# Diagonal matrices of x from a ring in DRAM in place of two engines' products

## The reference, cut to what matters

```python
xw = jnp.einsum('ntd,dh->nth', x, Wx) + b
def step(prev_h, xw_t):
    next_h = jnp.tanh(xw_t + prev_h @ Wh)
    return (next_h, next_h)
_, hs = jax.lax.scan(step, h0, jnp.swapaxes(xw, 0, 1))
```

## Time and profile before

| | us |
|---|---|
| median of 3 runs | 3383.85 |
| lowest and highest | 3377.65, 3384.16 |
| the profiled execution | 3381.28 |
| its span | 3379.5 |
| recurrence, first h_now to last | 12.8 to 2043.9 |
| VectorE busy | 2809.4 (83%) |
| GpSimd busy | 2593.7 (77%) |
| ScalarE busy | 2171.9 (64%) |
| TensorE busy | 2812.6 (83%) |

### The profile page before, as it was taken

How to read it: one execution, slowest core, us unless ns; L and a number is a source line. 1 busy time by engine, 2 the same in 40 slices (tenths; PEclk the granted TensorE clock), 3 DMA queues, 4 the chain that set the end, 5 groups by cost and what they waited for, 6 DMA issues and landing times.

```text
span 3379.5 us, 54177 instructions
## 1 busy us (share of the span) xinstructions
PE 2812.6 (83%) x12991; PEld 1717.5 (51%) x13101; DVE 2809.4 (83%) x8061; ACT 2171.9 (64%) x4492; POOL 2593.7 (77%) x2804
## 2 busy tenths in 40 slices
PE   5777778777787877878777788969999999999997
PEld 2333333333333333333333336746767777777676
DVE  5999999999999999999999994337777777777875
ACT  4666666666666666666666663336666666666665
POOL 8888888888888888888888881038778778778773
PEclk9999999999999999999999998879999999999999
DMA  1000000000000000000000002000010101000000
GB/s 33 0 0 0 0 0 0 0 0 0 0 0 0 0 0 0 0 0 0 0 0 0 0 0 73 1 1 1 0 36 0 36 0 36 0 32 4 0 0 7
DMA packets 21860, 21.97 MB, mean 7 GB/s; under 512 B 6334, under 2 KB 19396, under 8 KB 21060
## 3 DMA queue, kind: packets, MB, share of 16 engines
q1 hardware_dynamic: 21828, 21.55, 2.0%
HBM read 21.02 MB, written 0.52 MB: 6 GB/s over the span
## 4 chain that ended last, share of the span: by engine, by line
DVE 54%; PE 21%; issue 15%; ACT 4%; POOL 3%; DVEq 2%; SPq 0%; DMA 0%; POOLq 0%; ACTq 0%
DVE bank L1017 13%; PE bank L1322 5%; DVE bank L1012 3%; DVE bank L989 3%; DVE rot_s L1235 3%; DVE sq L989 3%; DVE rot_c L1235 3%; DVE ss L1238 3%; PE bank L1564 2%; DVE qT L998 2%; PE bank L1642 2%; DVE fix_trace L1083 2%; PE bank L1426 2%; PE bank L1616 2%; DVE sq L1075 2%
## 5 line engine op out<-in xcount | busy, mean ns | idle before, releaser
L1017 DVE TENSOR_REDUCE bank<-qkv_w 128x2 f32<-128x766 f32 (+1 forms) x768 | 912.7, 1219 | 120.6 <-issue 64.9
L739 ACT COPY qkv_w<-bank 128x512 f32<-128x512 f32 x258 | 218.2, 846 | 356.9 <-PE bank L1322 356.9
L667 POOL TENSOR_TENSOR qk<-rot_c,rot_s 128x512 f32<-128x512 f32 x192 | 256.8, 1337 | 207.8 <-DVE rot_s L1235 207.8
L1322 PE MATMUL bank<-diag_h,w_part 128*128 128x512 f32 x1024 | 307.2, 421 | 118.2 <-DVE bank L1012 106.9
L585 POOL TENSOR_TENSOR diag_h<-eye,part 128x512 fp32r<-128x512 f32 x384 | 393.9, 1040 | 0.0
L578 POOL TENSOR_TENSOR qkv_w<-b,offset 128x512 f32<-128x512 f32 x258 | 269.1, 1043 | 160.4 <-ACT b L721 150.0
L1327 PE MATMUL bank<-kT,wx 128*128 128x512 f32 x516 | 277.0, 618 | 136.3 <-ACT b L721 136.3
L1322 PE MATMUL bank<-diag_x,w_part 128*128 128x512 f32 x1032 | 385.6, 495 | 0.0
L1337 PE MATMUL bank<-qT,wh 128*128 128x256 f32 (+1 forms) x768 | 254.6, 467 | 95.6 <-DVE qT L998 95.6
L674 POOL TENSOR_TENSOR rs<-rs,halfs 128x8 f32<-128x8 f32 x192 | 320.1, 1667 | 16.0
L716 ACT ACTIVATE diag_x<-eye,X 128x128 fp32r<-128x128 f32 x1036 | 327.7, 389 | 1.4 <-DVE X L1110 1.4
(11 more groups left out here) (237 smaller groups left out, 6697.5 us busy)
## 6 DMA issues: line engine op xcount, KB each, us to landing
qkv_w<-in_L_ffn_Wqkv SPq DMA_DIRECT2D x6, 1536.0 KB
o_w<-in_L_ffn_Wo SPq DMA_DIRECT2D x6, 512.0 KB
w<-in_L_ffn_W SPq DMA_DIRECT2D x6, 341.0 KB
b<-in_L_ffn_b SPq DMA_DIRECT2D x6, 341.0 KB
w<-in_L_ffn_W SPq DMA_DIRECT2D x6, 128.0 KB
x_tok<-in_x SPq DMA_DIRECT2D x1, 512.0 KB
masks<-in_masks SPq DMA_DIRECT2D x1, 512.0 KB, 3.8
out<-o_fin SPq DMA_DIRECT2D x1, 512.0 KB, 3.2
```

What stands on the lines that cost most here:

```text
L667: pool.tensor_tensor(o, c_, s_[:, :, ::-1, :], ALU.add).then_inc(rot_sum, 1)
L1017: return dve.tensor_reduce((sum_h, sum_x)[n][:, a:b], chain[n][:, a:b, 0:LINKS], AX_X, ALU.add)
L1322: return pe.matmul(dst, w_part[:, n, w], diag[n][:, d, a:b, :].rearrange("p n k -> p (n k)"), start=start, stop=stop or n == 0, skip_group ...
```

## The change

`diag_x` is no longer computed. A tensor in DRAM, `diag_ring`, holds four slots of the tile's shape. VectorE clears the tile once, and SyncE stores the zeros to all four slots. Then, for a step of x, two DMAs write only the diagonals' elements, 128 x 8 for each part, 4 bytes at a time, a row of the tile and one column apart; the off-diagonal zeros stay. Two DMAs per step (one for each half of the batches, both parts at once, 512 KB) load a slot into `diag_x`. The first four steps are sent ahead of the loop, one after another; in the loop the sends run four steps ahead. ScalarE's and GpSimd's `diag_x` instructions go, in the prologue and in the loop, with the counters that found their slices. TensorE waits for the load of a half in place of the two engines.

```diff
+RING = 4
+        ring = nc.dram_tensor('diag_ring', (RING, P, 2, NB, D), F32, kind='Internal').ap()
@@ sync
+            def send_diagonals_x(step, slot):
+                for d in range(2):
+                    src = x_part[d][:, step, :] if isinstance(step, int) else x_part[d][:, bass.ds(step, 1), :].rearrange(
+                        "p a n -> p (a n)")
+                    dst = bass.AP(ring.tensor, (slot * P * 2 + d) * NB * D, [[2 * NB * D + 1, P], [D, NB], [1, 1]])
+                    sp.dma_start(dst, src.unsqueeze(2), allow_slow_non_contiguous=True).then_inc(diag_x_sent, 16)
+            def bring_diagonals_x(slot, half):
+                rows = slice(4 * half, 4 * half + 4)
+                sp.dma_start(diag[1][:, :, rows, :].bitcast(F32), ring[slot][:, :, rows, :]).then_inc(diag_x_ready[half], 16)
+            sp.wait_ge(diag_x_clear, 1)
+            for slot in range(RING):
+                sp.dma_start(ring[slot], diag[1].bitcast(F32)).then_inc(ring_clear, 16)
+            sp.wait_ge(x_split, 1)
+            sp.wait_ge(ring_clear, 16 * RING)
+            for slot in range(RING):
+                if slot:
+                    sp.wait_ge(diag_x_sent, 32 * slot)
+                send_diagonals_x(slot, slot)
+            for half in range(2):
+                bring_diagonals_x(0, half)
+            sp.wait_ge(rest_ready[1], 1)
+            bring_diagonals_x(1, 0)
+            with sp.Fori(0, T // RING) as turn:
+                for u in range(RING):
+                    t = RING * turn + u
+                    sp.wait_ge(rest_ready[1], value(sp, 2 * t + 2))
+                    bring_diagonals_x((u + 1) % RING, 1)
+                    sp.wait_ge(rest_ready[1], value(sp, 2 * t + 3))
+                    bring_diagonals_x((u + 2) % RING, 0)
+                    sp.wait_ge(diag_x_sent, value(sp, 32 * t + 32 * RING))
+                    send_diagonals_x(value(sp, (t + RING) % T), u)
@@ gpsimd
-            pool.wait_ge(x_split, 1)
-            for half in range(2):
-                diagonal(1, 1, half, lower_x(0, half), diag_x_ready[1])
...
-            pool.wait_ge(rest_ready[1], 1)
-            diagonal(1, 1, 0, lower_x(1, 0), diag_x_ready[1])
...
-                pool.wait_ge(rest_ready[1], counts[1])
-                diagonal(1, 1, 1, lower_x(around, 1), diag_x_ready[1])
...
-                pool.wait_ge(rest_ready[1], counts[2])
-                diagonal(1, 1, 0, lower_x(beyond, 0), diag_x_ready[1])
@@ scalar
-                diagonals_x(0, half)
-            diagonals_x(1, 0)
-                diagonals_x(around, 1)
-                diagonals_x(beyond, 0)
@@ vector
+            dve.memset(diag[1].rearrange("p a n k -> p (a n k)").bitcast(F32), 0.0).then_inc(diag_x_clear, 1)
@@ tensor
-            def rests_x(half, count):
+            def rests_x(half, count, landed):
...
+                pe.wait_ge(diag_x_ready[half], landed)
                 for d in range(2):
-                    pe.wait_ge(diag_x_ready[d], count)
                     times(at, 1, 0, d, a, b, False, False)
...
+            pe.wait_ge(diag_x_ready[0], 16 * T + 32)
+            pe.wait_ge(diag_x_sent, 32 * (T + RING))
```

More of the change, by code:

```diff
@@ L307, in program @@
         diag_lower_h = [sem("diag_lower_h%d" % half) for half in range(2)]
-        diag_x_ready = [sem("diag_upper_x"), sem("diag_lower_x")]
+        diag_x_ready = [sem("diag_x%d" % half) for half in range(2)]
+        diag_x_clear = sem("diag_x_clear")
+        diag_x_sent = sem("diag_x_sent")
+        ring_clear = sem("ring_clear")
         tri_h_first = sem("tri_h_first")
@@ L586, in diagonal @@
                                    values.unsqueeze(2).to_broadcast([P, 4, D]), ALU.mult).then_inc(done, 1)
-            def lower_x(m, half):
-                return x_part[1][:, m, 4 * half:4 * half + 4] if isinstance(m, int) else x_part[1][
-                    :, bass.ds(m, 1), 4 * half:4 * half + 4].rearrange("p a n -> p (a n)")
             def at_step(m):
@@ L611, in _ @@
                 counts = [value(pool, two + n) for n in (1, 2, 3, 4)]
-                around, beyond = (value(pool, (t + n) % T) for n in (1, 2))
                 pool.wait_ge(h_static, this)
@@ L711, in lower_h @@
                 ins.then_inc(diag_lower_h[0], 1)
[L713 to L717, removed]
             def take_sums_x(half, count):
@@ L761, in _ @@
                 counts = [value(act, two + n) for n in (1, 2, 3, 4)]
-                around, beyond = (value(act, (t + n) % T) for n in (1, 2))
                 place_guess_h(0, counts[0])
@@ L1364, in _ @@
             sums_x(1, 2)
-            rests_x(0, 1)
+            rests_x(0, 1, 16)
             pe.wait_ge(rest_placed[1], 1)
-            rests_x(1, 2)
+            rests_x(1, 2, 16)
             offset_h()
@@ L1371, in _ @@
                 counts = [value(pe, two + n) for n in (1, 2, 3, 4)]
+                landed = value(pe, 16 * t + 32)
                 for m in range(2):
@@ L1392, in _ @@
                 pe.wait_ge(rest_placed[1], counts[1])
-                rests_x(0, counts[2])
+                rests_x(0, counts[2], landed)
                 pe.wait_ge(guess_placed, counts[1])
@@ L1397, in _ @@
                 pe.wait_ge(rest_placed[1], counts[2])
-                rests_x(1, counts[3])
+                rests_x(1, counts[3], landed)
             def transposed(dst, src, cols, n, done):
```

## The result

| | before | after |
|---|---|---|
| median, us | 3383.85 (5 runs) | 3402.89 (5 runs) |
| lowest and highest | 3377.65, 3386.61 | 3395.32, 3405.14 |
| profiled execution, its span | 3381.28, 3379.5 | 3395.32, 3393.5 |
| first tanh scan, last tanh scan | 55.4, 2043.5 | 73.6, 2061.4 |
| TensorE's first matmul behind the recurrence | 2046.81 | 2064.95 |

The ratio is 1.0055, with a 95% interval of 1.0039 to 1.0070: slower by 0.55%, or 19.0 us between the medians. The profiled execution of after is the fastest of its five. Its recurrence ends 18.1 us later than before's (2064.95 against 2046.81), while its whole span is only 14.0 us longer. The other 4.1 us came back in the stages behind, whose code is the same, and the medians don't show that gain. The comparison is therefore made inside the recurrence.

A forecast was written before the change was run, and what follows sets the result against it. VectorE's row of instructions was taken to bound the loop, 14.69 of 15.67 us a turn. Prologue terms 12.4 - 0.3 + 2 = +14.1 us on the 3383.9 median gave 3398, range 3388 to 3424.

The forecast's parts named there:

- The steady turn: what goes: In the loop, ScalarE loses 2.54 us and GpSimd 2.08 us a turn; nobody on VectorE's row waits for either, value 0.
- The steady turn: what comes: In the loop, each turn's two 512 KB loads and the element sends stay hidden behind 14.2 us of cover, value 0.
- The stall bound: In the loop, traffic stops being hidden when a turn's sends take 12.7 us, or 99 ns a descriptor.
- The clears: In the prologue, four 1 MB stores of zeros start at 19.5 us, take 12.0 plus 0.5, and land at 32.0.
- A slot: In the prologue, each send waits for the landing before it and takes 3.3 us; three of them reach 41.9.
- The load: In the prologue, half 0's load takes 3.8 us, plus 0.6 behind the fourth send's elements, landing at 47.5.
- The slow matmuls: In the prologue, TensorE runs about half of its first rests slowly after some 12 us idle: +2 us (0 to 4).
- L716 out of the chain: In the prologue, ScalarE's 0.96 us `diag_x` instruction leaves the chain of waits: -0.3 us, between 0 and -1.0.
- The end: At the recurrence's end, the last sends, issued at about 2040, land within 5 us and delay the next stage by 0.
- Dear sends: Rival, chance 0.18: an element store costs 50 ns, 6.4 us a send; four on the prologue's path add 18 us, 3416.
- Ready sooner: Rival, chance 0.13: the prologue's ring is ready sooner, or scatter covers the delay; about +5 us, 3389.
- The loop gets faster: Rival, chance 0.07: GpSimd's `diag_x` products hold up VectorE's tanh; removing them returns 67 us over 128 turns, 3331.

The follow-up runs named there:

- e1: Kernel before, with the `diag_x` products of steps 1 to 127 left out on both engines and no ring; 3382.65 us, ratio 1.0005.
- e2: Kernel before with all its products, plus the whole ring traffic loaded into two unused tiles, TensorE waiting for the loads; 3401.98 us, ratio 1.0059.
- e6: Kernel after with seven further sends a turn into a tensor nobody reads, 8 in all; 4811.23 us, 26.48 us a turn.
- e7: Kernel after with eleven further sends a turn into a tensor nobody reads, 12 in all; 6203.24 us, 37.32 us a turn.
- e3: Kernel after, with step 0 sent and loaded before the other three slots are filled; 3389.63 us, ratio 1.0026.
- e5: Kernel after with zeros written first, ring DMAs issued ahead of later stages' loads, slot 0 first, last four sends dropped; 3384.91 us, ratio 1.0000.
- e4: Kernel after, with 17 extra matmuls keeping TensorE busy just ahead of its wait for the first load; 3399.42 us, ratio 1.0054.
- e12: Kernel of e8 with only the three tanh tiles `f_keep`, `f_guess` and `fix_keep` moved from PSUM to SBUF; 3801.48 us, ratio 1.1244.
- e10: Kernel of e8, no ring, with two more VectorE tanh instructions on ScalarE and three tanh tiles moved from PSUM to SBUF; 3741.39 us, ratio 1.1050.
- e9: Kernel of e5, the ring with the lean prologue, with VectorE's second h-triangle instruction made on ScalarE; 3340.40 us, ratio 0.9869.
- e8: Kernel before, no ring, with VectorE's second h-triangle instruction (0.33 us) made on ScalarE; 3341.78 us, ratio 0.9876.
- e11: Kernel of e9, with the ring, two more VectorE tanh instructions on ScalarE and three tanh tiles in SBUF; 3564.28 us, ratio 1.0533.

## Why the prediction was right

The time forecast, 3398.0, is 4.9 us under the median, inside the range and inside the likeliest case's own bounds (3394 to 3405).

**The steady turn: what goes is worth 0.** Right, and shown: e1 is 15.656 a turn with the products gone. ScalarE is at 8.28 where 8.0 was forecast, and GpSimd at 11.23 where 11.2 was.

**The steady turn: what comes costs 0.** Right, and shown by e2. The lengths inside the hidden part were too short. A load lands in 5.3 us, not 3.8, and an element costs 21 ns when the queues are full, not 14; both were within their cover of 14.2 us. The stall bound of 12.7 us of sends a turn was too high. At 2.7 us for a send, e6 and e7 both leave 4.8 us of their turns for all else, where the bound took 3.0. By them an old turn of 15.65 has room for 10.8 us, or four sends (an estimate; no run has between one and eight).

**The clears: 19.5 + 12.0 + 0.5 = 32.0.** Landed at 29.75. The stores ran at 387 GB/s where 350 was taken, and they were under way at the start of the window from 20 us, so that term was 2.2 too long.

**A slot: 3.3 us.** The first of two mis-sized terms. The sends are issued at 29.83, 34.42, 38.63 and 43.09, 4.4 us apart, so three cost 13.3 in place of 9.9. It was put together from a load into SBUF, which landed 2.3 us after its issue. The store into DRAM takes 3.8 to 4.1 from its second issue. The queues carry the first send's data until 32.1 us by their packets, and it lands at 34.40, 2.3 later: the greater part of the wait is behind the data.
The Trainium skill, page "DMA: Bandwidth & Descriptors", section "Anatomy of one DMA — SWDGE (gpsimd) path", says for another issuing path that most of some 2 us of fixed cost is the wait until the target memory confirms the last write, most of all in DRAM; the 2.3 us here agree in size.

**The load: 3.8 + 0.6.** The second mis-sized term: 6.91 us, +2.5. The load by itself is 4.4 (e3, with the second half's load behind it), 0.6 over the 3.8. The other 1.9 is in the 0.6 for the fourth send's elements ahead of it: they cost 6.91 - 4.43 = 2.5. The loads issued right behind a send in e2 and e5 take 6.90 and 6.91 too, and e5's first one, issued when its send had landed, 4.4.

**Together.** First rests at 51.09 and not 47.5: +16.0 where +12.4 was forecast. The errors are -2.2 for the clears, +3.4 for the three slots, -0.2 for the fourth's issue and +2.5 for the load, in all +3.5.

**The slow matmuls: +2 (0 to 4).** 2.9, measured alone by e4. **L716 out of the chain: -0.3.** Right. From the end of the last rests to ScalarE's next copy 1.88 us pass before (40.43 to 42.31) and 1.63 in after (58.87 to 60.50), since the h sums then take L716's place; e1, without the ring, has the same 1.63. What is left of the first scan's 18.2 is 18.2 - 16.0 - 2.9 = -0.7, so -0.4 more. It comes from the start 35.09: there the four matmuls overlap with those before them and take 1.50 us, and from a standing start they take 1.14 (e4). **The end: 0.** Some 0.2, since the last sends land 6.2 us after their issue and not within 5.

**The sum.** 16.0 + 2.9 - 0.7 = 18.2 against 14.1, and 19.0 between the medians. Of the 4.1 us missing in the first, 3.6 are transfers that were priced by rows of transfers in other company or going the other way; 0.9 are the clock's, and -0.4 is that overlap. Luck had a part in the nearness: the clears came 2.2 sooner than forecast, against 5.9 too little for the sends and the load. The profiled spans differ by 14.0 us, next to the 14.1 forecast, and that is chance, since 4.1 us of the delay came back behind the recurrence.

**The rivals.** *Dear sends*: the price for each element with full queues, 21 ns, was in the range kept (9 to 25), and 50 is excluded by e6 and e7. *Ready sooner*: excluded by the row at 51.09; it takes e5's other order of issues to get there. *The loop gets faster*: the mechanism exists and the reason given against it was half of the matter. L1017, which isn't held up, has one SBUF input and writes PSUM; no run moved it. In the tanh each instruction with two inputs reads one of them from PSUM (`bank`), and that is what keeps it free. Beside the same GpSimd products, with `f_keep` and `f_guess` in SBUF, it is held up by 0.70 to 0.85 us at a time (e12).
The Trainium skill, page "SBUF — State Buffer", section "SBUF: two separate sides", calls the shared pair of ports an exclusive lock that whoever starts first holds for the whole instruction. e10's equal ends agree. It names instructions with two SBUF inputs and those in a 2-port mode. `den_upper<-f_guess`, with a single input and 1004 ns, would have to be of the second kind. No run here tells that apart: e10's `z_upper<-f_keep`, of the same form, starts 0.01 us behind a product and takes 0.16.

## What to carry to other kernels

Work taken off engines that wait for another one is worth nothing: 4.2 us a turn less on ScalarE and GpSimd gave none (e1), and none either when VectorE's row was 0.33 us shorter (e9 against e8). That 0.33 us itself gave 42 us (e8). A set-up of DMAs that each wait for the one before costs 4 us a step on the path, so send first what the first turn needs and issue it ahead of the loads that can wait (e3, e5). Small element stores right ahead of a load that is waited for cost it another 2.5 us (after against e3). Before a tile is moved from PSUM to SBUF, look for GpSimd products beside the VectorE instructions that read it.

## What the runs showed of the hardware

- Stores of single 4-byte elements from SBUF to DRAM cost 1.355 us for each 1024 when the queues are full (21 ns each on one of 16 engines), while a burst of 2048 shows 7 ns a packet and lands 3.8 to 4.1 us after its second issue (e6, e7, after).
- A load of 512 KB lands in 4.4 us with an equal one behind it and in 6.9 when 2048 such elements were issued just ahead (e3, after).
- The first three groups of matmuls took 5.9 us at a granted clock of 0.50, after 15.6 us of idle, and 3.1 us at 1.00 when TensorE had been kept busy (after, e4). After 2.62 us of idle the first group took 1.21 at 1.00, in place of 2.09 (e3).
- With their inputs in SBUF, three of VectorE's 128x8 instructions last until the GpSimd product beside them ends: 0.87 to 1.00 us in place of 0.16 (e10, e12). TensorE, left waiting 3.29 us and not 0.74, then took 3.48 us for six matmuls and not 1.99, at a granted clock of 0.50 at first (e12); after 2.23 us it took 1.99 at 1.00 (e11).
